# Attention over 16 groups of four heads: row maxima reduced two PSUM banks at a time, value products issued in parts of at most 256 columns

## The chip, the cores and the metric

The kernel runs on one core of one Trainium2 chip. A time is the device time of one launch in microseconds, a median over repeated runs. A profile is one execution of the same program recorded by the hardware profiler; its times below are microseconds from the first instruction.

## The reference, cut to what matters

The whole kernel is a two-layer transformer (attention with a feed-forward gate, then a retention layer with a gated mixture of experts). The change lies in the attention of the first layer, for 4 batches of 1024 tokens and 16 heads of width 8:

```python
S = 1024; NUM_HEADS = 16; D_K = 8
scores = einsum('bhnd,bhmd->bhnm', Q, K) / sqrt(D_K)      # Q, K with rotary positions
scores = where(tril(ones((S, S))), scores, -inf)
attn = softmax(scores, axis=-1)
head = einsum('bhnm,bhmd->bhnd', attn, V)
```

## The kernel before

Attention is one block with a hand-written order for each engine. Heads are taken four at a time: 16 groups x = 0 to 15 (4 batches, 4 quads of heads), pipelined over one another.

A softmax needs the maximum of each row before the exponentials. The kernel computes every score twice. First, `for_maximum` multiplies queries by keys with queries on the partitions, and VectorE (DVE) reduces each PSUM bank of up to 512 columns to one maximum a row (L766). A group has 40 such units; 8 of them hold two narrow heads in a bank. Then GpSimd (POOL) splits the negated maxima into two bf16 parts, TensorE (PE) turns them over (`turn_over`, L874), they are copied to SBUF as `negB` (L756) and placed by DMA as two extra rows of the queries (`place`). Second, `for_products` multiplies keys by queries with the keys on the partitions; the extra rows subtract the maxima inside the matmul. ScalarE (ACT) takes the exponential of that bank (L854) into the ring `probs`, which PE multiplies with the values (`products`, L959). A group has 40 such steps e = 0 to 39, in 12 slots j of (half c of the queries, key tile jt). Slots on the diagonal get four more small matmuls a head that add a mask (L899, L928); "masked" below means those.

PE interleaves the two kinds: each step issues one bank of scores for the exponentials (L921) together with one bank for the maxima of a later group (L892), in opposite halves of the array (`side_by_side`). So step e of group x stands beside unit e + 16 of group x + 1, or beside unit e - 24 of group x + 2 from e = 24 on. Widths match: 512 columns at steps 0 to 3, 12 to 23, 28 to 31 and 36 to 39, 384 at 4 to 7 and 24 to 27, and two heads of 128 or 256 columns at 8 to 11 and 32 to 35. Steps 0 to 11, 20 to 27 and 32 to 35 are masked.

PSUM has eight banks. Four (`mxb`, `RING`) take turns for the maxima, three (`st`, `BANKS`) for the exponentials, and one (`pv`) collects the value products of all four heads:

```python
LAG, DEEP = 5, 16
if n >= RING:
    pe.wait_ge(max_read, n - RING + 1)     # for_maximum: DVE has read this bank
if n >= BANKS:
    pe.wait_ge(exp_done, n - BANKS + 1)    # for_products: ACT has read this bank
```

`products(x, j)` is one block of four fp32 matmuls for slot j, as wide as the slot (512, 384, 256 or 128 columns), issued `LAG` steps after the slot's last step. A fp32 matmul is two records in the profile, so a block shows as x8. The 12 blocks of a group follow steps 0, 4, 7, 12, 14, 16, 20, 24, 28, 31, 36 and 38 (those after 0 and 4 belong to the group before). When a half of the queries is complete, ACT copies `pv` out (`keep`, L841): after the exponential of step 16, and of step 4 for the previous group. The first product block of the next half (slot 4 after step 20, slot 0 after step 7) waits for that copy (`out_kept`).

Before group 0 there are 44 units of maxima alone and a turn-over, then 12 more units. After group 13 maxima are left for one group only, and group 15 has none; small work of the second layer (`output_projection`, `turn_rows`) stands inside it.

Of the kernel before, what the change touches and what calls it, by code (L numbers as in the profile page):

```python
# [23 lines left out]
ACT = mybir.ActivationFunctionType  # L24
AX = mybir.AxisListType

P = 128
# [561 lines left out]
def attention(nc, A, groups, second, kept_until):  # L589
# [24 lines left out]
    LAG, DEEP = 5, 16  # L614
# [8 lines left out]
    order = prologue + [u for x in range(NQ) for u in stream(x)]  # L623
    place_of = {u: n for n, u in enumerate(order)}

# [9 lines left out]
    with Space(nc) as m:  # L635
        ps = m.psum("psB")
        mxb = [ps[:, i, :] for i in range(RING)]
# [26 lines left out]
        with nc.Block() as block:  # L664
            @block.sync
            def _(sp):
# [40 lines left out]
                sp.wait_ge(max_read, place_of[0, None] + 1)  # L707
                place(0)
                for x in range(NQ):
# [7 lines left out]
                    if x + 1 < NQ:  # L717
                        sp.wait_ge(max_read, place_of[x + 1, None] + 1)
# [21 lines left out]
            def _(dve):  # L740
# [4 lines left out]
                for n, (x, g) in enumerate(order):  # L745
                    if n == AHEAD:
# [3 lines left out]
                    if (x, g) == (SCALED, None):  # L750
                        reciprocals(0)
                    dve.wait_ge(max_done, n + 1)
                    if g is None:
                        if x >= 2:
                            dve.wait_ge(neg_placed[par], PLACED * (x // 2))
                        nc.vector.tensor_copy(neg[:, par, :], mxb[n % RING][0:64, 0:P]).then_inc(max_read, 1)  # L756
                        continue
                    heads, t, c = units[g]
                    w = max_width(t, c)
                    table, col = (mx, t) if c == 0 else (mx2, t - 4)  # L760
                    if len(heads) == 1:
                        dst, src = table[:, par, heads[0] % 2, heads[0] // 2, col:col + 1], mxb[n % RING][:, 0:w]
                    else:
                        dst = table[:, par, heads[0] % 2, :, col]
                        src = mxb[n % RING][:, 0:2 * w].rearrange("p (a w) -> p a w", w=w)
                    nc.vector.tensor_reduce(dst, src, AX.X, ALU.max).then_inc(max_read, 1)  # L766
                    if g == UNITS - 1:
                        dve.wait_ge(max_read, n + 1)
# [67 lines left out]
            def _(act):  # L836
# [5 lines left out]

                act.wait_ge(g2["in_loaded"], 16)
                nc.scalar.activation(second.gate[:, :, :], second.u[:, :, :], ACT.Silu).then_inc(g2["gated"], 1)
                act.wait_ge(g2["init"], 2)
                nc.scalar.activation(second.warm[:, :], second.eps[:, :], ACT.Exp)
                for x in range(NQ):
                    for e, (j, heads) in enumerate(steps):
                        n = UNITS * x + e
                        w = slot_width(j) * len(heads)  # L850
                        if n >= DEEP:
                            act.wait_ge(pv_done, read_up_to(n - DEEP))
                        act.wait_ge(st_done, n + 1)
# [1463 lines left out]
```

## Time and profile before

| | us |
|---|---|
| median of 3 runs | 1017.38 |
| lowest, highest | 1016.93, 1026.69 |
| span of the profiled execution | 1008.0 |
| median less span | 9.4 |
| attention, maxima of group 0 to the last copy | 117.5 to 539.2 |
| one group in the steady part | 23.84 |

The profiled execution has no time of its own beside the span; the 9.4 us are what lies around it by the median. The attention block is 42% of the span. The rest of the program is not touched.

### The profile page before, as it was taken

What the parts mean: (1) busy time and instruction counts of PE and PEld (TensorE: products, weight loads), DVE (VectorE), ACT (ScalarE), POOL (GpSimd) and SP (SyncE); (2) the same over time, 40 slices, a digit from 0 to 9 for tenths busy, and PEclk for the clock granted to TensorE, in tenths of its full rate; (3) what the DMA queues carried; (4) which work ended last, traced back from release to release, by engine and by line L of the source; (5) the groups of instructions that cost most, each with busy time, mean ns of one, the idle gap of its engine ahead of it and who ended that gap; (6) DMA issues with size and microseconds to landing.
All of it is one profiled execution on the core that took longest, in us unless ns stands there. A gap on an engine that the chain in (4) does not pass through costs nothing. (4 is left out here: it accounts for less than half of the span.)

```text
span 1008.0 us, 25094 instructions
## 1 busy us (share of the span) xinstructions
PE 874.2 (87%) x9373; PEld 464.7 (46%) x9374; DVE 816.2 (81%) x1699; ACT 725.7 (72%) x1493; POOL 289.1 (29%) x331
## 2 busy tenths in 40 slices
PE   4999899899999999999898898778999999979960
PEld 3666543334333333333344666533444444458850
DVE  6665499899999999999923766589999999928895
ACT  2666408788888888888784454478999999948851
POOL 4865311111111000000003656500344443005560
PEclk9999859999999999999999888768999999989995
DMA  5579851644445353330004899695354643546637
GB/s 167 223 267 331 280 133 42 205 101 105 110 98 125 89 123 84 68 69 14 13 24 127 277 317 301 226 241 101 67 118 94 114 89 54 136 142 189 206 119 252
DMA packets 121560, 147.20 MB, mean 146 GB/s; under 512 B 19213, under 2 KB 81242, under 8 KB 120800
## 3 DMA queue, kind: packets, MB, share of 16 engines
q1 hardware_dynamic: 116064, 133.74, 48.0%
q0 software_dynamic: 5376, 11.85, 4.1%
q8 instruction: 76, 1.25, 0.5%
q14 instruction: 44, 0.36, 0.1%
HBM read 77.63 MB, written 69.54 MB: 146 GB/s over the span
## 5 line engine op out<-in xcount | busy, mean ns | idle before, releaser
L854 ACT ACTIVATE probsB<-psB 128x512 f32<-128x512 f32 (+2 forms) x640 | 310.0, 566 | 87.1 <-PE psB L928 61.5
L766 DVE TENSOR_REDUCE mxB<-psB 128x1 f32<-128x512 f32 (+2 forms) x448 | 256.9, 642 | 11.1 <-PE psB L892 8.3
L921 PE MATMUL psB<-q_groups,k_groups 64*128 64x512 bf16 (+3 forms) x768 | 205.8, 330 | 16.6 <-DVE mxB L766 8.3
L892 PE MATMUL psB<-k_groups,q_groups 64*128 64x512 bf16 (+3 forms) x768 | 217.0, 344 | 2.8 <-PEq L293 1.7
L959 PE MATMUL psB<-probsB,vB 128*32 128x512 f32 (+3 forms) x1536 | 164.5, 500 | 0.7 <-ACT probsB L854 0.5
L1725 ACT ACTIVATE psD<-psD 128x896 f32<-128x896 f32 (+2 forms) x192 | 153.4, 799 | 12.9 <-PE psD L1779 12.7
L921 PEld LDWEIGHTS psB<-q_groups,k_groups 64*128 64x128 bf16 x768 | 67.5, 94 | 161.2 <-ACT probsB L854 140.3
L1656 DVE TENSOR_REDUCE sumsD<-psD 128x1 f32<-128x128 f32 (+3 forms) x256 | 113.2, 481 | 11.8 <-PE psD L1802 9.4
L899 PE MATMUL psB<-hideB,chooseB 64*128 64x128 bf16 (+1 forms) x1024 | 115.1, 210 | 0.0
L1779 PE MATMUL psD<-k_groups,q_groups 64*128 64x512 bf16 (+3 forms) x384 | 104.4, 343 | 12.3 <-ACT psD L1725 5.6
L766 DVE TENSOR_REDUCE mx2B<-psB 128x1 f32<-128x384 f32 (+2 forms) x192 | 104.4, 594 | 8.5 <-PE psB L899 6.9
L928 PE MATMUL psB<-hide_laterB,chooseB 64*128 64x64 bf16 (+1 forms) x1024 | 109.7, 205 | 0.0
L815 POOL TENSOR_SCALAR partsB<-mxB 128x32 f32<-128x32 f32 x16 | 4.6, 290 | 346.7 <-DVE mxB L769 346.7
L928 PEld LDWEIGHTS psB<-hide_laterB,chooseB 64*128 64x128 bf16 x1024 | 88.6, 95 | 19.8 <-issue 1.4
L899 PEld LDWEIGHTS psB<-hideB,chooseB 64*128 64x128 bf16 x1024 | 92.2, 98 | 9.9 <-issue 3.9
L1711 POOL DMA_INDIRECT slot_x<-xD,indexR x64 | 64.4, 1006 | 77.8 <-DVE sumsD L1656 39.5
L1667 DVE TENSOR_TENSOR keptD<-psD,causalD 128x512 f32<-128x512 f32 x128 | 82.5, 680 | 0.3 <-PE psD L1798 0.2
L892 PEld LDWEIGHTS psB<-k_groups,q_groups 64*128 64x128 bf16 x768 | 69.0, 95 | 13.4 <-DVE mxB L766 9.2
L1960 POOL DMA_INDIRECT back<-zE,toE x40 | 44.3, 1107 | 86.8 <-DVE zE L2147 76.7
L1779 PEld LDWEIGHTS psD<-k_groups,q_groups 64*128 64x128 bf16 x384 | 29.8, 96 | 80.8 <-ACT psD L1725 47.4
L1802 PE MATMUL psD<-k_groups,q_groups 64*128 64x128 bf16 (+3 forms) x256 | 64.8, 314 | 0.9 <-DVE keptD L1667 0.9
L1798 PE MATMUL psD<-q_groups,k_groups 64*128 64x128 bf16 x512 | 49.0, 225 | 6.8 <-DVE sumsD L1656 6.2
(227 smaller groups left out, 1504.5 us busy)
## 6 DMA issues: line engine op xcount, KB each, us to landing
v<-vaugA SPq DMA_DIRECT2D x4, 2048.0 KB, 8.9
vB<-v SPq DMA_DIRECT2D x16, 512.0 KB
q_groups<-q SPq DMA_DIRECT2D x32, 200.0 KB
k_groups<-k SPq DMA_DIRECT2D x32, 200.0 KB
q_groups<-q SPq DMA_DIRECT2D x32, 192.0 KB
k_groups<-k SPq DMA_DIRECT2D x32, 192.0 KB
back<-emptyB POOLq DMA_DIRECT2D x16, 256.0 KB, 3.8
o<-outB SPq DMA_DIRECT2D x128, 32.0 KB, 1.8
```

Of the source, the lines that this page charges most:

```text
L766: nc.vector.tensor_reduce(dst, src, AX.X, ALU.max).then_inc(max_read, 1)
L854: nc.scalar.activation(probs[:, n % DEEP, 0:w], st[n % BANKS][:, 0:w], ACT.Exp, scale=DH ** -0.5).then_inc(exp_done, 1)
L892: ins = nc.tensor.matmul(bank[:, to:to + w], q[half[r], s, hq // 2, t * P:t * P + P], k[half[r], s, hq // 2, HALF * c:HALF * c + w], start ...
L899: ins = nc.tensor.matmul(bank[:, to - P + ROWS * part:to], choose[half[r], part, :], hide[half[r], part, ROWS * part:P], start=False, stop ...
L921: ins = nc.tensor.matmul(bank[:, to:to + w], k[half[r], s, hq // 2, jt * P:jt * P + P], q[half[r], s, hq // 2, i0:i0 + w], start=True, sto ...
L928: ins = nc.tensor.matmul(bank[:, to:to + ROWS * (part + 1)], choose[half[r], part, :], hide_later[half[r], part, 0:ROWS * (part + 1)], sta ...
L959: ins = nc.tensor.matmul(pv[VW * hq:VW * hq + VW, HALF - w:HALF], v[:, s, jt, VW * hq:VW * hq + VW], probs[:, (UNITS * x + at) % DEEP, to: ...
L1656: ins = V.tensor_reduce(sums[:, s, unit:unit + 1], src[:, at:at + P * t], AX.X, ALU.add, apply_absolute_value=True)
L1667: V.tensor_tensor(dst[:, :, :, half, :], piece_bank[n % PIECE_RING].rearrange("p (t a i) -> p t a i", t=2, a=2), causal[:, None, None, :]. ...
L1725: nc.scalar.activation(src, src, ACT.Abs, accum_out=sums[:, s, unit:unit + 1]).then_inc(score_read, 1)
L1779: ins = nc.tensor.matmul(score[n % SCORE_RING][:, cols], q[r, s, hq // 2, P * t:P * t + P], k[r, s, hq // 2, cols], start=True, stop=True)
L1802: ins = nc.tensor.matmul(bank[:, at:at + P * t], q[r, s, hq // 2, P * t:P * t + P], k[r, s, hq // 2, 0:P * t], start=True, stop=True)
```

## The change

- Two maxima banks form a slot of the ring. `for_maximum` waits for a slot at its first bank only; DVE makes one reduction over both banks (20 a group for 40), and frees both at once.
- `turn_over` writes into the ring of the exponentials (`st`, three banks) and no longer into that of the maxima. Its copy to `negB` moves from DVE to ACT, `keep_negated`, in front of the exponential of step 28. Semaphore counts follow (`st_place`).
- A slot's products come in parts of at most 256 columns: 512 as two of 256, 384 as two of 192. That makes 20 blocks a group for 12. They follow the odd steps, one a pair of steps, from the fourth step after a slot's last one on (`LAG` 4): 256 columns after steps 1, 3, 5, 7, 9, 17, 19, 21, 23, 25, 27, 29, 35 and 37; 192 after 11, 13, 31 and 33; 128 after 15 and 39.
- `keep` now stands after the exponentials of steps 17 and 5. The first block of the next half follows steps 19 and 7 and waits for `out_kept` as before.

```diff
-    LAG, DEEP = 5, 16
+    SLOT = 2
+    LAG, DEEP, PART = 4, 16, HALF // 2
+    chunks = [(j, i, -(-slot_width(j) // PART)) for j in range(SLOTS_B) for i in range(-(-slot_width(j) // PART))]
+    issue_at, free = [], 1
+    for j, _, _ in chunks:
+        at = max(free, last_step[j] + LAG)
+        issue_at.append(at)
+        free = at + 2
+    HALF_AT = max(at for at, (j, _, _) in zip(issue_at, chunks) if j == 3)
+    END_AT = issue_at[-1] - UNITS
...
-        mxb = [ps[:, i, :] for i in range(RING)]
+        mxb = ps[:, 0:RING, :]
...
-                    dve.wait_ge(max_done, n + 1)
-                    if g is None:
-                        if x >= 2:
-                            dve.wait_ge(neg_placed[par], PLACED * (x // 2))
-                        nc.vector.tensor_copy(neg[:, par, :], mxb[n % RING][0:64, 0:P]).then_inc(max_read, 1)
-                        continue
+                    dve.wait_ge(max_done, SLOT * (m + 1))
...
+                    both = mxb[:, SLOT * m % RING:SLOT * m % RING + SLOT, :]
...
-                        dst, src = table[:, par, heads[0] % 2, heads[0] // 2, col:col + 1], mxb[n % RING][:, 0:w]
+                        dst, src = table[:, par, :, heads[0] // 2, col], both[:, :, 0:w]
...
+                def keep_negated(x):
+                    at = st_place[x, None]
+                    if x >= 2:
+                        act.wait_ge(neg_placed[x % 2], PLACED * (x // 2))
+                    act.wait_ge(st_done, at + 1)
+                    nc.scalar.copy(neg[:, x % 2, :], st[at % BANKS][0:64, 0:P]).then_inc(exp_done, 1)
...
-                        if e == last_step[3] + LAG:
+                        if e == HALF_AT:
                             keep(x, 0)
-                        if e == LAG - 1 and x:
+                        if e == END_AT and x:
                             keep(x - 1, 1)
...
-                    if n >= RING:
-                        pe.wait_ge(max_read, n - RING + 1)
+                    if n >= RING and n % SLOT == 0:
+                        pe.wait_ge(max_read, (n - RING) // SLOT + 1)
...
-                def products(x, j):
+                def products(x, j, i, parts_of):
...
+                    part = w // parts_of
+                    if i == 0:
+                        pe.wait_ge(exp_done, st_place[x, last_step[j]] + 1)
...
+                        if jt == 0 and x + c:
+                            pe.wait_ge(out_kept, 2 * x + c)
...
-                        if waiting and due(*waiting[0]) <= UNITS * x + e:
-                            products(*waiting.pop(0))
+                        if due[0][0] == UNITS * x + e:
+                            products(*due.pop(0)[1])
```

On PE, at steps 15 to 20 of a group in the steady part (L921 and L892 are the two scores of a step, L959 the products), the order before is:

```order
L959 MATMUL psB<-probsB,vB 32x128 x4
L921 MATMUL psB<-q_groups,k_groups 128x512
L892 MATMUL psB<-k_groups,q_groups 128x512
L921 MATMUL psB<-q_groups,k_groups 128x512
L892 MATMUL psB<-k_groups,q_groups 128x512
L959 MATMUL psB<-probsB,vB 32x256 x4
L921 MATMUL psB<-q_groups,k_groups 128x512
L892 MATMUL psB<-k_groups,q_groups 128x512
L921 MATMUL psB<-q_groups,k_groups 128x512
L892 MATMUL psB<-k_groups,q_groups 128x512
L921 MATMUL psB<-q_groups,k_groups 128x512
L892 MATMUL psB<-k_groups,q_groups 128x512
```

and after the change, from step 16 on (L947, L918 and L988 are the lines that were L921, L892 and L959):

```order
L988 MATMUL psB<-probsB,vB 32x128 x4
L947 MATMUL psB<-q_groups,k_groups 128x512
L918 MATMUL psB<-k_groups,q_groups 128x512
L947 MATMUL psB<-q_groups,k_groups 128x512
L918 MATMUL psB<-k_groups,q_groups 128x512
L988 MATMUL psB<-probsB,vB 32x256 x4
L947 MATMUL psB<-q_groups,k_groups 128x512
L918 MATMUL psB<-k_groups,q_groups 128x512
L947 MATMUL psB<-q_groups,k_groups 128x512
L918 MATMUL psB<-k_groups,q_groups 128x512
L988 MATMUL psB<-probsB,vB 32x256 x4
```

Before, three steps follow the block of slot 3 and a fourth (masked) comes before the block of 512 columns of slot 4; after, a block stands behind every second step, and the first half of slot 4 stands two steps behind slot 3.

On ACT, from step 20 of one group to step 19 of the next (L841 is `keep`), before:

```order
L854 ACTIVATE probsB<-psB 128x512 x10
L854 ACTIVATE probsB<-psB 128x384
L841 COPY outB<-psB 128x512
L854 ACTIVATE probsB<-psB 128x384 x3
L854 ACTIVATE probsB<-psB 128x256 x2
L854 ACTIVATE probsB<-psB 128x512 x7
L841 COPY outB<-psB 128x512
L854 ACTIVATE probsB<-psB 128x512 x7
```

and after (L879 the exponentials, L856 `keep`, L863 `keep_negated`):

```order
L879 ACTIVATE probsB<-psB 128x512 x10
L879 ACTIVATE probsB<-psB 128x384 x2
L856 COPY outB<-psB 128x512
L879 ACTIVATE probsB<-psB 128x384 x2
L879 ACTIVATE probsB<-psB 128x256 x2
L879 ACTIVATE probsB<-psB 128x512 x8
L856 COPY outB<-psB 128x512
L879 ACTIVATE probsB<-psB 128x512 x6
L879 ACTIVATE probsB<-psB 128x384 x4
L863 CAST negB<-psB 64x128
```

Each `keep` stands one exponential later, and the copy of the negated maxima is now in this queue, behind the 384-wide exponentials of steps 24 to 27.

## Rows read from the trace of the kernel before

**Rows 1.** The page, part 1, one engine: busy time, share, instructions.

```profile
PE 874.2 (87%) x9373; PEld 464.7 (46%) x9374; DVE 816.2 (81%) x1699; ACT 725.7 (72%) x1493; POOL 289.1 (29%) x331
```

**Rows 2.** Busy time, PE clock, DMA in four stretches.

```profile
core 0: us, PE busy (x) PEld busy (x) DVE busy (x) ACT busy (x) POOL busy (x), PEclk, DMA share, GB/s
125.00:140.00 15.00, 14.47 (x75) 6.47 (x74) 14.91 (x29) 0.00 (x0) 0.00 (x0) 0.50 0.76 178
...
286.10:310.00 23.90, 22.45 (x322) 9.19 (x322) 22.67 (x44) 20.21 (x43) 3.36 (x8) 1.00 0.46 106
...
500.60:538.60 38.00, 35.19 (x333) 14.26 (x333) 10.07 (x34) 28.35 (x60) 1.87 (x2) 0.96 0.33 90
```

**Rows 3.** The turn-over (L874) by tile: count, durations ns, first and last start.

```profile
L874 PE MATMUL psB<-identC,partsB x11: 270/271/272, 238.4 to 476.8; 128*64 128x128 f32 x11
```

**Rows 4.** Waits of one group, 262.3 to 286.1: total, times, longest.

```profile
PEld psB L921 <- ACT probsB L854: 9.0, 14, 0.9
```

**Rows 5.** DVE: four reductions in a row (timeline), and a 1024-element reduction (groups).

```profile
311.40 2.46 DVE L766 TENSOR_REDUCE mxB<-psB 128x1 f32<-128x512 f32 x4
...
L2095 DVE TENSOR_REDUCE msE<-sqE 128x128 f32<-128x1024 f32 x4 | 4.9, 1220 | 0.1
```

**Rows 6.** Timeline of PE, steps 15 to 20: start, us, instructions.

```profile
277.63 0.42 PE L959 MATMUL psB<-probsB,vB 128*32 128x128 f32 x8
277.99 0.39 PE L921 MATMUL psB<-q_groups,k_groups 64*128 64x512 bf16 x1
...
278.23 0.39 PE L921 MATMUL psB<-q_groups,k_groups 64*128 64x512 bf16 x1
...
278.55 0.64 PE L959 MATMUL psB<-probsB,vB 128*32 128x256 f32 x8
279.12 0.39 PE L921 MATMUL psB<-q_groups,k_groups 64*128 64x512 bf16 x1
...
279.35 0.73 PE L921 MATMUL psB<-q_groups,k_groups 64*128 64x512 bf16 x2
279.70 0.39 PE L892 MATMUL psB<-k_groups,q_groups 64*128 64x512 bf16 x1
280.68 0.39 PE L921 MATMUL psB<-q_groups,k_groups 64*128 64x512 bf16 x1 [0.59 <-DVE mxB L766]
```

**Rows 7.** Timeline of ACT over the same steps.

```profile
277.58 2.06 ACT L854 ACTIVATE probsB<-psB 128x512 f32<-128x512 f32 x4 [0.17 <-PE psB L921]
279.50 0.62 ACT L841 COPY outB<-psB 128x512 f32<-128x512 f32 x1
279.97 2.13 ACT L854 ACTIVATE probsB<-psB 128x512 f32<-128x512 f32 x4
```

**Rows 8.** Timeline, steps 3 and 4; then steps 21 to 27 and the turn-over.

```profile
270.79 0.38 PE L921 MATMUL psB<-q_groups,k_groups 64*128 64x512 bf16 x1
...
271.40 0.33 PE L921 MATMUL psB<-q_groups,k_groups 64*128 64x384 bf16 x1
...
282.08 0.39 PE L921 MATMUL psB<-q_groups,k_groups 64*128 64x512 bf16 x1
...
282.65 1.96 ACT L854 ACTIVATE probsB<-psB 128x512 f32<-128x512 f32 x4 [0.56 <-PE psB L928]
...
282.69 0.38 PE L921 MATMUL psB<-q_groups,k_groups 64*128 64x512 bf16 x1
...
283.30 0.33 PE L921 MATMUL psB<-q_groups,k_groups 64*128 64x384 bf16 x1
...
283.65 1.07 PE L959 MATMUL psB<-probsB,vB 128*32 128x512 f32 x8
284.55 0.17 DVE L769 TENSOR_TENSOR mxB<-mxB,mx2B 128x16 f32<-128x16 f32 x1
...
284.65 0.33 PE L921 MATMUL psB<-q_groups,k_groups 64*128 64x384 bf16 x1
...
285.16 0.32 PE L921 MATMUL psB<-q_groups,k_groups 64*128 64x384 bf16 x1
...
286.12 0.27 PE L874 MATMUL psB<-identC,partsB 128*64 128x128 f32 x1 [0.55 <-ACT probsB L854]
```

More of the change, by code:

```diff
@@ L613, in attention @@
     RING, BANKS = 4, 3
-    LAG, DEEP = 5, 16
+    SLOT = 2
[6 more added lines that the diff above has]
+        free = at + 2
+    assert all(at % 2 for at in issue_at) and issue_at[0] + UNITS >= free
+    HALF_AT = max(at for at, (j, _, _) in zip(issue_at, chunks) if j == 3)
+    END_AT = issue_at[-1] - UNITS
     def stream(x):
@@ L622, in attention @@
     prologue = [(0, g) for g in range(AHEAD)] + stream(-1)
-    order = prologue + [u for x in range(NQ) for u in stream(x)]
+    sequence = prologue + [u for x in range(NQ) for u in stream(x)]
+    order = [u for u in sequence if u[1] is not None]
     place_of = {u: n for n, u in enumerate(order)}
+    st_order = [(0, None)]
+    for x in range(NQ):
+        turned_at = next((e for e, u in enumerate(stream(x)) if u[1] is None), None)
+        for e in range(UNITS):
+            st_order += [(x + 1, None)] * (e == turned_at) + [(x, e)]
+    st_place = {u: n for n, u in enumerate(st_order)}
     def offset(heads, hq, w):
@@ L743, in reciprocals @@
                     nc.vector.reciprocal(second.rden[:, b, :], second.den[:, b, :]).then_inc(g2["rden_ready"], 1)
-                for n, (x, g) in enumerate(order):
-                    if n == AHEAD:
+                for m in range(len(order) // SLOT):
+                    x, g = order[SLOT * m]
+                    if SLOT * m == AHEAD:
                         nc.vector.memset(empty[:, :, 0:D + 1], 0.0).then_inc(emptied, 1)
@@ L846, in _ @@
                 nc.scalar.activation(second.warm[:, :], second.eps[:, :], ACT.Exp)
+                keep_negated(0)
                 for x in range(NQ):
                     for e, (j, heads) in enumerate(steps):
[L849 removed]
+                        n, at = UNITS * x + e, st_place[x, e]
                         w = slot_width(j) * len(heads)
+                        if st_order[at - 1] == (x + 1, None):
+                            keep_negated(x + 1)
                         if n >= DEEP:
                             act.wait_ge(pv_done, read_up_to(n - DEEP))
[L853 to L854 removed]
+                        act.wait_ge(st_done, at + 1)
+                        nc.scalar.activation(probs[:, n % DEEP, 0:w], st[at % BANKS][:, 0:w], ACT.Exp,
                                              scale=DH ** -0.5).then_inc(exp_done, 1)
[L856 removed]
+                        if e == HALF_AT:
                             keep(x, 0)
[L858 removed]
+                        if e == END_AT and x:
                             keep(x - 1, 1)
@@ L912, in for_products @@
                     w = slot_width(j)
[L913 removed]
+                    n = st_place[x, e]
                     if n >= BANKS:
@@ L991, in _ @@
                         side_by_side(for_maximum(x, g))
-                waiting = []
+                due = [(UNITS * x + at, (x, *chunk)) for x in range(NQ) for at, chunk in zip(issue_at, chunks)]
                 for x in range(NQ):
@@ L996, in _ @@
                     for e, (j, heads) in enumerate(steps):
-                        both = [for_products(x, e)]
                         if todo and todo[0][1] is None:
                             turn_over(todo.pop(0)[0])
+                        both = [for_products(x, e)]
                         if todo:
@@ L1011, in _ @@
                     assert not todo
-                for y in waiting:
-                    products(*y)
+                for _, chunk in due:
+                    products(*chunk)
 def between_layers(nc, A, groups, L, second, order, kept_until):
```

50 lines of the change are left out of this document (21 added, 29 removed).

## The prediction, made before the changed kernel ran

> **What bounds the kernel now.** The page comes first: no engine is full over the span, PE is fullest at 87% [rows 1]. The change lies in the attention, so the busy times by stretch come next. One steady group shows PE busy 22.45 of 23.90 us, DVE 22.67, ACT 20.21, at the full clock of 2.4 GHz [rows 2]. Two engines look full, and from this view alone one would take DVE, whose instructions are cut by half, for the bound. The turn-overs give the period: 11 of them from 238.4 to 476.8, 23.84 us a group [rows 3]. The list of waits names ACT 14 times a group in front of PE's loads of weights [rows 4], but a load idles there while a product block still streams, so those 9.0 us are no measure. What decides is the distance between starts on PE, compared with what the same piece takes when nothing holds it.
>
> The pieces are regular. An unmasked step takes 0.23 us (279.12 to 279.35) [rows 6]; two masked ones of 512 take 0.61 (282.08 to 282.69) [rows 8]. A product block of 128 columns takes 0.36 (277.63 to 277.99), one of 256 takes 0.57 (278.55 to 279.12), one of 512 takes 1.00 (283.65 to 284.65) [rows 6, 8]. That is a line: 0.145 us plus 0.00167 a column, so 0.465 for 192 and 0.785 for 384. The step in front of a block takes 0.32 and not 0.23 (278.23 to 278.55) [rows 6], so getting into a block costs 0.09 more.
>
> Against these times a group has about 2.6 us in which PE stands still. 0.87 of it lies at the copy `keep`: step 18 takes 0.35 and step 19 0.98 (279.70 to 280.68) where 0.23 would do each [rows 6], since ACT spends the time from 279.50 to 279.97 on the copy and frees the three banks late [rows 7]. 0.31 lies at step 23, which takes 0.61 (282.69 to 283.30): ACT had run dry during a block of 512, starts step 21's bank 0.57 after PE began it, and needs about 0.6 more. 0.31 lies at step 3 in the same way (270.79 to 271.40). 0.71 lies at the turn-over, where step 27 takes 0.96 (285.16 to 286.12) and the two before it 0.51 together (284.65 to 285.16) [rows 8], because the chain of last reduction, combination, POOL is late. The starts of the group's other steps leave some 0.4 in pieces of at most 0.1, of which 0.25 lie at steps 38 to 2, again behind a block of 512. So PE's own work is about 23.84 - 2.6 = 21.2 us a group. **DVE holds PE up only at the turn-over.** Four reductions of 512 take 2.46 us, last one 0.68, so they start 0.593 apart [rows 5]; over the 40 of mixed widths that is 21.6 us, under the period.
>
> **The change part by part, a steady group.**
> DVE: a pair of 512 takes 1.19 us now. A reduction of 1024 elements takes 1.22 and not 2 x 0.68 [rows 5]; its start-to-start should be 0.085 less, as for the small ones, 1.13. So one pair saves 0.06 us, 20 pairs 1.2 us, and a small copy goes as well. DVE drops to some 20.4 us. This reduction reads SBUF; that two PSUM banks cost the same is not in the trace. Bounds: 1.07 (the slope alone) and 1.36 (two full durations). I take 1.13. All of it lies beside PE's work and is worth nothing by itself.
> The Trainium skill, VectorE: DVE Perf Modes, section on the TRN2 errata, gives a PSUM read a fixed 120 cycles, 0.125 us an instruction; by it 20 fewer would save 2.5 us and not 1.2. The trace's spacing of 0.593 for 512 columns speaks for 0.06, and even 2.5 would be hidden in the same way.
>
> Products: 12 blocks sum to 6 x 1.00 + 2 x 0.785 + 2 x 0.57 + 2 x 0.36 = 9.43 us. 20 blocks are 14 x 0.57 + 4 x 0.465 + 2 x 0.36 = 10.56. That is +1.13, and eight more changes from scores to products at 0.10 (0.09 into it, 0.01 on the first step after it) give +0.8. Together **+1.95 us a group on PE**, with nothing to hide it, since PE sets the period. 192 and the second half of a slot are no rows of the trace; bounds +1.6 and +2.3.
> The Trainium skill, TensorE: Matmul & The Clock Gate, Part 2, says that loads of weights are pulled ahead of running matmuls. If the edges of a block were hidden so, the split would be free; what it would give is a rival below. The trace speaks against it, with 0.145 us of every block that no column accounts for.
>
> Stalls. With a block of at most 256 behind every second step, an unmasked pair lasts 0.23 + 0.32 + 0.57 = 1.11 us, a masked one about 1.26. ACT starts a bank some 0.48 us after PE does (0.57 masked) and holds it 0.60, at 0.48 apart [rows 7, 8]: the third step from it needs the bank 1.3 us or more after, it is free at 1.14 to 1.23. So both 0.31 stalls go (-0.62) and those of steps 38 to 2 (-0.25). At the turn-over, step 23 starts at t; the pair's reduction starts at t + 0.54, ends at t + 1.75, and the chain needs 1.57 more (284.55 to 286.12) [rows 8]: t + 3.36. PE is there at t + 3.32, since four blocks now lie between. So -0.66 of the 0.71.
> At `keep` after step 17, with step 16 at T: the exponential of 17 starts at T + 0.96, the copy at T + 1.44, and ends at T + 2.04 (0.47 behind the exponential, 0.60 long) [rows 7]. The block behind step 19 waits for it and would be ready at T + 1.65. That is a **new wait** of 0.44 us on PE, and all later steps queue behind it. In the run before it, pairs with blocks of 128 and 192 take PE 0.9 to 1.0 us where DVE needs 1.13, so PE meets a slot not yet read, 0.15 in all. 0.87 becomes 0.59: -0.28. `keep` after step 5 does the same with 384-wide banks: block ready at 1.77, copy done at 2.0: +0.25 where there was no stall. `keep_negated` costs ACT some 0.3 us of its 3 us of slack; one bank of `st` is gone for a step, and step 30 comes 0.6 us after the copy is done: nothing.
>
> Sum: +1.95 - 0.62 - 0.25 - 0.66 - 0.28 + 0.25 = **+0.39 us a group**, 24.2 us. Over the 14 periods with all three kinds of work, +5.4 us.
>
> **Prologue and end.** 56 units run alone at half clock, 1.2 GHz, with DVE busy 14.91 of 15 us [rows 2]: DVE is the bound there. 28 pairs save 0.06 each, 1.7 us; the first reduction waits for a second bank and the last is longer (+0.7): -1.0. In the last 38 us PE has scores of one kind alone, ACT is busy 28.35 us [rows 2]; 11 more blocks cost 2.6 us and blocks of 256 stop ACT running dry, worth 1 to 4 us. I take 0. Sum: +4.4 us on the span of 1008.0, so 1012.4; with the 9.4 around it 1021.8 against 1017.38. The rest of the program is not touched.
>
> **The rivals.**
> *New waits add up (slower).* Every place where I count a wait of 0.1 to 0.4 rests on 0.05 to 0.2 us of slack. If the copies of both halves come one exponential later than reckoned (+0.48 each), or the slot of two banks is freed late at the 10 unmasked pairs (0.07 each), a group takes 0.7 to 1.7 more: 25.2, +1.4 x 14 = 19, so 1036. For it: the chain ACT, PE, ACT is visible at every `keep` [rows 6, 7]. Against: ACT and DVE each get 3 us of slack. It is slower by 1% from +0.7 a group on.
> *The waits vanish.* If the copy starts as soon as its block is done, and no slot is late, the group is 21.2 + 1.95 + 0.15 = 23.3: -0.5 x 14 = -8 us, 1009.
> *The split is free.* Then 21.2 and about 0.9 of waits: 22.1, -1.7 x 14 = -24 us and so 993. Only this case needs a fixed cost that the trace shows 12 times a group to go away.
> *DVE was the bound after all.* PE's stalls would then be DVE's doing, and the period falls with DVE's work, by 1.5 to 2: 22.1, 993. Against: the stalls sit where ACT is late, and DVE falls idle in the same group for 1.2 us.
> *It does not do what it says*: the order shows 20 blocks and 20 reductions a group, so this has no chance of its own.
>
> **How the numbers follow.** Forecast (+1 to +9) 0.58; new waits 0.25; waits vanish 0.10; free split 0.04; DVE the bound 0.03. A measurement of this kernel tells 1%, 10 us, from no change. Of the forecast some 0.05 lies above 1%, of the vanishing waits 0.03 below: faster 0.10, same 0.61, slower 0.29. The range takes in the bounds of the split (-5 and +5), the vanishing waits and the nearer half of the new waits: 1006 to 1034.
>
> **What would show it.** Right: products of 256 columns 0.57 us from start to start; turn-overs 24.2 apart; step 27 no longer long; a gap of 0.4 us in front of the block behind step 19, released by the copy; DVE busy about 20.5 a group with its idle time doubled or more. Wrong: turn-overs under 23.5 apart (split cheaper, or no waits), or DVE still busy 22 us (two banks read more slowly). The whole would be wrong if the clock did not stay at full rate in the groups, which nothing in the change suggests.

## The result, and the profile after

The change makes the kernel slower: 1032.63 us (median of 4 runs, 1029.57 to 1037.07) against 1020.06 before in the same rounds. The ratio is 1.0144, interval 1.0100 to 1.0188. Run again later beside other kernels (e9) it was 1.0151, interval 1.0106 to 1.0196. The prediction, 1021.8 in a range of 1006 to 1034, was too low: it had +4.4 us where the medians differ by 12.6 and the ratio makes 14.6. Its chance for "slower by over 1%" was 0.29.

The profiled execution has a span of 1031.8 us, 23.8 more than the one before. Less than that is the change's. Cut at the first score of the maxima and the end of the last copy of the products, the two traces give:

| stretch, us | before | after | difference | forecast |
|---|---|---|---|---|
| start to the first score (untouched) | 117.47 | 119.44 | +2.0 | 0 |
| first score to the first turn-over | 24.47 | 24.85 | +0.4 | -1.0 |
| first to last turn-over, 15 periods | 358.7 | 371.2 | +12.5 | +5.4 |
| last turn-over to the last copy | 38.5 | 39.4 | +0.8 | 0 |
| the rest of the program (untouched) | 468.8 | 477.0 | +8.2 | 0 |

The attention takes 13.7 us more, which agrees with the 14.6 us that 1.0144 makes. The untouched rest is not constant from one profiled execution to the next: over the profiles of this study it took 467.8 to 479.5 us. So spans of single profiles are no measure here, and below the distances between turn-overs are read instead. A run also lasts 1.8 us more than its span (1033.61 and 1031.8), not the 9.4 that the prediction put around it: the profiled execution before was simply a quick one.

First the page of the changed kernel, part 1:

```profile
PE 889.8 (86%) x10397; PEld 481.6 (47%) x10398; DVE 800.8 (78%) x1363; ACT 737.7 (71%) x1509; POOL 289.3 (28%) x331
```

Against [rows 1], PE has 1024 matmuls more and is busy 15.6 us longer. DVE has 336 instructions fewer and is busy only 15.4 us less. By stretches (columns as in [rows 2]):

```profile
125.00:140.00 15.00, 9.06 (x68) 3.74 (x66) 13.95 (x15) 1.61 (x3) 0.00 (x0) 0.50 0.90 206
286.00:310.00 24.00, 23.36 (x381) 10.17 (x384) 21.00 (x21) 20.39 (x43) 3.31 (x7) 1.00 0.44 101
```

In a steady stretch of 24 us PE is now busy 23.36 us where it was 22.45 in 23.90 [rows 2], and DVE 21.00 where it was 22.67. The roles are clear: PE is full, DVE is not. The turn-over's line by tile (columns as in [rows 3]):

```profile
L900 PE MATMUL psB<-identC,partsB x16: 298/298/423, 144.3 to 515.5; 128*64 128x128 f32 x16
```

and of DVE's groups by form (count, busy us, mean ns, idle before them) the widest:

```profile
L781 DVE TENSOR_REDUCE mxB<-psB 128x2 f32<-128x1024 f32 x148 | 172.8, 1219 | 6.5 <-PE psB L918 4.9 <-PE psB L925 1.4
```

The turn-overs from 144.3 to 515.5 are 24.75 us apart on average; ten of the fifteen distances are 24.56 to 24.61, and the first three, the eighth and the last are longer, 24.82 to 25.65. Steady period: **24.56 us for 23.84**. A reduction of two banks takes 1.219 us, what a 1024-element one took in SBUF [rows 5].

The timeline of PE at steps 14 to 20, to be held against [rows 6]:

```profile
309.34 0.37 PE L947 MATMUL psB<-q_groups,k_groups 64*128 64x512 bf16 x1
...
309.88 0.43 PE L988 MATMUL psB<-probsB,vB 128*32 128x128 f32 x8
310.47 0.37 PE L947 MATMUL psB<-q_groups,k_groups 64*128 64x512 bf16 x1 [0.17 <-ACT probsB L879]
...
311.01 0.64 PE L988 MATMUL psB<-probsB,vB 128*32 128x256 f32 x8
311.61 0.37 PE L947 MATMUL psB<-q_groups,k_groups 64*128 64x512 bf16 x1
...
311.84 0.38 PE L947 MATMUL psB<-q_groups,k_groups 64*128 64x512 bf16 x1
312.65 0.64 PE L988 MATMUL psB<-probsB,vB 128*32 128x256 f32 x8 [0.44 <-ACT outB L856]
313.22 0.39 PE L947 MATMUL psB<-q_groups,k_groups 64*128 64x512 bf16 x1
```

Two gaps stand out. The block of 128 columns is followed by step 16 after 0.59 us (309.88 to 310.47), where it was 0.36. And the block behind step 19 starts 0.81 us after the step's first score (311.84 to 312.65), where 0.31 is normal: PE waits for `keep`. DVE and ACT at the same place:

```profile
309.11 4.61 DVE L781 TENSOR_REDUCE mxB<-psB 128x2 f32<-128x1024 f32 x4
...
309.81 2.22 ACT L879 ACTIVATE probsB<-psB 128x512 f32<-128x512 f32 x4
311.91 0.59 ACT L856 COPY outB<-psB 128x512 f32<-128x512 f32 x1
312.38 1.12 ACT L879 ACTIVATE probsB<-psB 128x512 f32<-128x512 f32 x2
```

Four two-bank reductions take 4.61 us, so they start 1.13 apart, and the first ends at 310.33. Step 16 needs that slot and starts 0.14 later. (The row of step 16 names ACT. The exponential whose bank step 16 takes is that of step 13, three banks back, and it had ended at 309.86; with single banks, in e2, this wait is gone.) The copy runs from 311.91 to 312.50, and the block starts 0.15 after it.

The turn-over is where the wait went away. In the changed kernel it follows a block, without a gap (the block of 256 takes its 0.57 us, 317.55 to 318.12):

```profile
317.55 0.64 PE L988 MATMUL psB<-probsB,vB 128*32 128x256 f32 x8
318.12 0.30 PE L900 MATMUL psB<-identC,partsB 128*64 128x128 f32 x1
```

### The profile page after: what moved, and what is told of

It is laid out like the page before. It is cut to its first block and busy times, and to the rows that moved or that the text cites. A ratio compares the mean times of both kernels' runs of the same rounds, so it can differ in the third digit from the quotient of the medians.

```text
span 1031.8 us, 26531 instructions
## 1 busy us (share of the span) xinstructions
PE 889.8 (86%) x10397; PEld 481.6 (47%) x10398; DVE 800.8 (78%) x1363; ACT 737.7 (71%) x1509; POOL 289.3 (28%) x331
## 5 line engine op out<-in xcount | busy, mean ns | idle before, releaser
L879 ACT ACTIVATE probsB<-psB 128x512 f32<-128x512 f32 (+2 forms) x640 | 318.9, 556 | 67.6 <-PE psB L954 55.9
L781 DVE TENSOR_REDUCE mxB<-psB 128x2 f32<-128x1024 f32 (+2 forms) x224 | 244.9, 1143 | 19.2 <-PE psB L925 13.1
L918 PE MATMUL psB<-k_groups,q_groups 64*128 64x512 bf16 (+3 forms) x768 | 205.4, 342 | 13.1 <-DVE mxB L781 9.5
L947 PE MATMUL psB<-q_groups,k_groups 64*128 64x512 bf16 (+3 forms) x768 | 207.2, 330 | 5.3 <-ACT probsB L879 3.0
L988 PE MATMUL psB<-probsB,vB 128*32 128x256 f32 (+2 forms) x2560 | 191.9, 372 | 11.0 <-ACT outB L856 10.7
L781 DVE TENSOR_REDUCE mx2B<-psB 128x2 f32<-128x768 f32 (+2 forms) x96 | 100.5, 1048 | 29.4 <-PE psB L925 28.4
L947 PEld LDWEIGHTS psB<-q_groups,k_groups 64*128 64x128 bf16 x768 | 64.9, 94 | 122.7 <-ACT probsB L879 101.4
L1803 PE MATMUL psD<-k_groups,q_groups 64*128 64x512 bf16 (+3 forms) x384 | 106.1, 350 | 11.7 <-ACT psD L1749 3.6
L925 PE MATMUL psB<-hideB,chooseB 64*128 64x128 bf16 (+1 forms) x1024 | 110.8, 210 | 0.0
L925 PEld LDWEIGHTS psB<-hideB,chooseB 64*128 64x128 bf16 x1024 | 88.3, 98 | 13.9 <-issue 2.2
L988 PEld LDWEIGHTS psB<-probsB,vB 128*32 128x32 f32 x2560 | 51.6, 108 | 78.6 <-ACT probsB L879 40.3
L918 PEld LDWEIGHTS psB<-k_groups,q_groups 64*128 64x128 bf16 x768 | 63.0, 95 | 20.8 <-DVE mxB L781 15.3
```

What stands on the lines that cost most here:

```text
L879: nc.scalar.activation(probs[:, n % DEEP, 0:w], st[at % BANKS][:, 0:w], ACT.Exp, scale=DH ** -0.5).then_inc(exp_done, 1)
L918: ins = nc.tensor.matmul(bank[:, to:to + w], q[half[r], s, hq // 2, t * P:t * P + P], k[half[r], s, hq // 2, HALF * c:HALF * c + w], start ...
L925: ins = nc.tensor.matmul(bank[:, to - P + ROWS * part:to], choose[half[r], part, :], hide[half[r], part, ROWS * part:P], start=False, stop ...
L947: ins = nc.tensor.matmul(bank[:, to:to + w], k[half[r], s, hq // 2, jt * P:jt * P + P], q[half[r], s, hq // 2, i0:i0 + w], start=True, sto ...
L988: ins = nc.tensor.matmul(pv[VW * hq:VW * hq + VW, col:col + part], v[:, s, jt, VW * hq:VW * hq + VW], probs[:, (UNITS * x + at) % DEEP, to ...
L1803: ins = nc.tensor.matmul(score[n % SCORE_RING][:, cols], q[r, s, hq // 2, P * t:P * t + P], k[r, s, hq // 2, cols], start=True, stop=True)
```

## The experiments

Each is told with its steady period, read as the distance between turn-overs in its profile, which is the same within 0.02 us over seven or more groups. The time of whole runs stands beside it. The median of the kernel before was 1012.33 in the rounds of e1 to e4, 1017.88 in those of e5 to e8 and 1018.92 in those of e9 to e11, so only ratios are compared across them. The ratios of e2 to e5 lie within one another's intervals, and e3's 1.0099 against 1.0144 is more than its period explains; what sets the variants apart from one another is read from the periods, and the ratios say only that each is slower or faster than the kernel before. e6, e7 and e8 ran once each.

| kernel | maxima | product blocks | period, us | attention, us | ratio to before (interval) |
|---|---|---|---|---|---|
| before | one bank | 12, whole | 23.84 | 421.7 | |
| changed | two banks | 20, parts | 24.56 | 435.4 | 1.0144 (1.0100 to 1.0188) |
| e1 | two banks | 12, whole, odd steps | 24.89 | 441.7 | 1.0201 (1.0143 to 1.0259) |
| e2 | one bank | 20, parts | 24.30 | 428.5 | 1.0106 (1.0074 to 1.0138) |
| e3 | two banks | 20, parts, copy first | 24.48 | 435.1 | 1.0099 (1.0072 to 1.0127) |
| e4 | two banks | 18 | 24.37 | 435.4 | 1.0093 (1.0065 to 1.0121) |
| e5 | one bank | 12, whole, odd steps | 24.31 | 433.1 | 1.0104 (1.0062 to 1.0145) |
| e6 | one bank | 12, in adjacent parts | 23.88 | 422.6 | one run, 1018.0 us |
| e7 | one bank, half read | 12, whole | 23.47 | 411.1 | one run, 1004.0 us |
| e8 | two banks | 20, parts, short copy | 23.98 | 429.8 | one run, 1023.6 us |
| e9 | two banks | 20, parts (changed again) | 24.57 | 434.9 | 1.0151 (1.0106 to 1.0196) |
| e10 | one bank | 12, turn-over at 30 | 23.57 | 419.5 | 0.9973 (0.9947 to 0.9999) |
| e11 | one bank | 12, turn-over at 32 | 23.59 | 416.6 | 0.9963 (0.9937 to 0.9989) |

### e1: product blocks whole again

```diff
-    LAG, DEEP, PART = 4, 16, HALF // 2
+    LAG, DEEP, PART = 4, 16, HALF
```

> The changed kernel with the value products whole again (12 blocks a group, up to 512 columns, behind odd steps), all else as in the change. Theory A (the split is what costs: PE has 23.3 us of its own work a group, 8 more blocks of 0.24 us each, and the copy waits): PE's own work falls to about 21.3 us, the turn-overs come 22.3 to 23.0 us apart for 24.56, and the time falls about 25 us below the changed kernel's, to below the kernel before. Theory B (the slots of two banks cost, since PE waits until both are read): the turn-overs stay at 24 us or more, since a pair of steps without a block now runs into a slot that is still being read.

The period rose to 24.89 us and the time to 1.0201. Theory A, that taking the parts back would give the 2 us of block edges back, is refuted for this arrangement. Its timeline of PE shows where the time goes, at steps 0 to 3:

```profile
300.49 0.37 PE L947 MATMUL psB<-q_groups,k_groups 64*128 64x512 bf16 x1
...
300.81 0.38 PE L947 MATMUL psB<-q_groups,k_groups 64*128 64x512 bf16 x1
...
301.63 0.37 PE L947 MATMUL psB<-q_groups,k_groups 64*128 64x512 bf16 x1 [0.35 <-DVE mxB L781]
```

Step 1 takes 0.82 us (300.81 to 301.63) for 0.30, and the release is DVE's. A pair without a block behind it lasts 0.6 us on PE, and DVE needs 1.13 for the pair before. The parts do add work to PE, but with slots of two banks they also spread PE's work so that it runs into fewer of DVE's reads.

### e2: maxima one bank at a time

```diff
-    SLOT = 2
+    SLOT = 1
-        bank = mxb[:, n // SLOT * SLOT % RING + heads[0] % 2, :]
+        bank = mxb[:, n % RING, :]
```

and one reduction a bank, as in the kernel before.

> The changed kernel with maxima reduced one bank at a time (40 reductions a group), the products in parts and the turn-over in the ring of the exponentials as in the change. Theory A: PE's blocks and the two waits for the copy stay, so the turn-overs come 24.3 to 24.7 us apart, as in the changed kernel, though DVE is busy some 1.2 us a group more. Theory B: without two-bank slots the 0.3 to 0.4 us of waits in front of steps 14 to 18 go and the period is 24.2 or less. If DVE's work mattered by itself (theory C, DVE a second bound), the period would rise to 25 or more.

24.30 us, against 24.56. So reading in pairs costs 0.26 us a group and gains nothing, though DVE does more work in e2. The number lies in theory A's range, and the 0.26 are theory B's mechanism: the two do not exclude one another. Theory C falls. The pieces show the waits for a slot gone: the block of 128 columns behind step 15 is followed by step 16 after 0.36 us again (309.25 to 309.61), and the gap in front of the block of step 19 is 0.6 us, the largest of the group:

```profile
310.98 0.38 PE L948 MATMUL psB<-q_groups,k_groups 64*128 64x512 bf16 x1
311.89 0.42 PE L989 MATMUL psB<-probsB,vB 128*32 128x256 f32 x4 [0.54 <-ACT outB L857]
```

The parts, with their new places and the turn-over in the other ring, cost 24.30 - 23.84 = 0.46 us.

### e3: the copy in front of the exponential

```diff
+                        if e == HALF_AT:
+                            keep(x, 0)
+                        if e == END_AT and x:
+                            keep(x - 1, 1)
                         act.wait_ge(st_done, at + 1)
                         nc.scalar.activation(probs[:, n % DEEP, 0:w], st[at % BANKS][:, 0:w], ACT.Exp,
                                              scale=DH ** -0.5).then_inc(exp_done, 1)
-                        if e == HALF_AT:
-                            keep(x, 0)
-                        if e == END_AT and x:
-                            keep(x - 1, 1)
```

> The changed kernel with the copy of the products (keep) in front of the exponential of steps 17 and 5 on ScalarE, where it stood behind it. Theory A: the copy starts when its block is done, 0.25 us sooner at step 17 and 0.15 sooner at step 5, so the gap in front of the block of step 19 falls from 0.52 to about 0.25 us and the one of step 7 from 0.27 to about 0.1: period 24.56 - 0.4 = 24.15 us, 6 us in all. If the gap is not the copy's doing, the period stays at 24.56.

The period fell to 24.48, by 0.08 and not 0.4. The gap at step 19 did shrink, from 0.50 to 0.35 us:

```profile
311.33 0.38 PE L947 MATMUL psB<-q_groups,k_groups 64*128 64x512 bf16 x1
311.99 0.64 PE L988 MATMUL psB<-probsB,vB 128*32 128x256 f32 x8 [0.28 <-ACT outB L856]
```

That of step 7 grew by 0.05, since ACT now stands idle 0.34 us until its block is done. The copy cannot start before the block is out of PE; its place in ACT's queue was a small part of the wait. The mechanism is right, its size was overrated.

### e4: only the blocks of 512 in parts

```diff
+    parts_in = [2 if slot_width(j) == HALF else 1 for j in range(SLOTS_B)]
-    chunks = [(j, i, -(-slot_width(j) // PART)) for j in range(SLOTS_B) for i in range(-(-slot_width(j) // PART))]
+    chunks = [(j, i, parts_in[j]) for j in range(SLOTS_B) for i in range(parts_in[j])]
```

> The changed kernel with the blocks of 384 columns whole and only those of 512 in two parts: 18 blocks a group for 20. The first block of slot 4 then still follows step 19, but the copy stands behind step 15. Theory A: 2 x 0.24 us less of PE's own work, and the wait of 0.52 us for the copy at step 19 goes: 24.56 - 1.0 = 23.55 us a group, 15 us less than the changed kernel. If edges of blocks cost nothing (the products' columns alone count), only the 0.5 of the wait goes: 24.05.

24.37 us, 0.19 less than the changed kernel and not 1.0. The wait of the block for the copy is gone, but another took its place at once:

```profile
312.71 0.38 PE L948 MATMUL psB<-q_groups,k_groups 64*128 64x512 bf16 x1
313.61 0.37 PE L948 MATMUL psB<-q_groups,k_groups 64*128 64x512 bf16 x1 [0.52 <-DVE mxB L782]
```

Steps 16 to 18 now come with no block behind 17, so step 17 takes 0.90 us and step 18 another 0.40. ACT's row shows the copy in that place, at 312.84 for 0.62 us, with the exponentials that should free banks behind it. Two waits overlap here. Step 18 itself waits for DVE: its slot of two banks is read until 0.14 us before it starts, while the exponential that it needs, of step 15, had ended 0.6 us before. Step 19 then waits for the exponential behind the copy. The second wait would stand without the first: in e5, with single banks, steps 17 and 18 take 0.35 and 0.98, 1.33 us for the 1.30 here. So the time lost is that of the stall of the kernel before [rows 6], back in a new place.

Over the whole attention e4's profile shows no gain on the changed kernel (435.4 us both): one of its distances between turn-overs is 28.44 us, with the granted clock at half for 3.4 us of it, where the changed kernel has 25.65.

### e5: one bank at a time and blocks whole

e1 and e2 together.

> The changed kernel with both parts undone but its placement kept: maxima one bank at a time, products whole, behind odd steps, and the turn-over in the ring of the exponentials. With e1, e2 and the changed kernel it makes a square of two by two. If paired reading costs through PE's waits for a slot and the parts are what hides them, the square shows an interaction: this kernel's period lies near the kernel before (23.84 us), 23.2 to 23.9, far under e1's 24.89. If the placement at odd steps is what is bad about e1, the period stays above 24.5. If it is under 23.6, this version beats both kernels.

24.31 us. With e1, e2 and the changed kernel it completes the square:

| period, us | 12 blocks whole | 20 blocks in parts |
|---|---|---|
| one bank | 24.31 | 24.30 |
| two banks | 24.89 | 24.56 |

Pairs cost 0.58 us with whole blocks and 0.26 with parts. At these odd places the parts cost nothing in the end: they add 2 us to PE's work and take 2 us of its waits. The 0.47 us to the kernel before's 23.84 lie in what all four share: blocks at odd steps with LAG 4, and the turn-over with its copy among the exponentials. No run has one without the other, but e5's timeline tells where the time is:

```profile
275.31 0.32 PE L948 MATMUL psB<-q_groups,k_groups 64*128 64x384 bf16 x1
...
275.97 0.33 PE L948 MATMUL psB<-q_groups,k_groups 64*128 64x384 bf16 x1 [0.25 <-ACT probsB L880]
...
289.98 0.63 PE L948 MATMUL psB<-q_groups,k_groups 64*128 64x512 bf16 x2
...
290.88 0.39 PE L948 MATMUL psB<-q_groups,k_groups 64*128 64x512 bf16 x1 [0.27 <-ACT probsB L880]
```

Step 6 takes 0.66 us (275.31 to 275.97) for 0.24, and step 30 takes 0.66 for 0.23: the fourth step since a block, 7 and 31, starts late, as steps 4 and 24 do in the kernel before [rows 8]. At their old places the whole blocks leave four runs of four wide steps (512 or 384 columns), at the odd ones six. The two new stalls are +0.85 us; the wait in front of the turn-over shrinks by 0.41, from step 27's 0.96 to step 26's stall of 0.31; every other stall of the kernel before stands within 0.03 us, some a step earlier. That makes up the 0.47, so in e5 it is the placing; the turn-over in its new ring shows no wait of its own. That the period would lie at 23.2 to 23.9 did not hold; that pairs and whole blocks harm one another did.

### e6: the parts directly behind one another

```diff
+                    parts_of = 2 if w > HALF // 2 else 1
+                    part = w // parts_of
+                    for i in range(parts_of):
                         for hq in range(4):
```

in `products` of the kernel before, with columns and flags as in the change.

> The kernel before with each product block of 512 or 384 columns issued as two parts directly behind one another, no scores between: the instructions of the change's parts without its moves. If the fixed cost of a block (0.145 us) is paid at the change between scores and products, an adjacent second part adds at most 0.05 us: 8 x 0.05 = 0.4 us at most, period 23.8 to 24.2. If it is a cost of every eight matmuls with their loads of weights, each adds 0.145: 8 x 0.145 = 1.2, period about 24.9.

23.88 us for 23.84. A block of 512 in two adjacent parts takes 1.01 us (292.90 to 293.91), as the whole one did:

```profile
292.90 1.07 PE L963 MATMUL psB<-probsB,vB 128*32 128x256 f32 x16
293.91 0.39 PE L921 MATMUL psB<-q_groups,k_groups 64*128 64x512 bf16 x1
```

So eight more matmul records with their loads of weights cost nothing. The 0.145 us of a block that no column accounts for is paid once for products that stand together, so at the change between products and scores. The Trainium skill, TensorEngine Tiling (Array Packing), Key Properties, says that changing the tiling mode drains TensorE. The trace agrees so far as each change has a price, some 0.24 us for a block's way in and out. That the price is such a drain is not shown: products and scores differ in their rows (128 and 64) and in their type (fp32 and bf16), and no run changes one alone.

### e7: half of DVE's work

```diff
-                        dst, src = table[...], mxb[n % RING][:, 0:w]
+                        dst, src = table[...], mxb[n % RING][:, 0:w // 2]
```

in the kernel before, the packed units likewise, with the exponential's scale at a thousandth.

> The kernel before with VectorE reducing only the left half of each bank (the maxima are of half the columns, and the exponential's scale is a thousandth, so the output is not the attention's; all instructions and waits stay). It takes about half of DVE's work away, 11 us a group. If DVE is not the bound (the prediction's reading), only the wait at the turn-over goes, 0.71 us: period 23.1. If DVE's work was the bound or helped to set it, the period falls to 22.3 or less, and the worth of the 20 reductions saved was more than nothing.

DVE's busy time fell to 15.49 us in 24, and the period from 23.84 to 23.47 only:

```profile
286.00:310.00 24.00, 22.98 (x335) 9.44 (x333) 15.49 (x44) 20.51 (x44) 3.31 (x7) 1.00 0.47 108
```

Every piece of PE's group is as it was within 0.03 us but one, the step in front of the turn-over:

```profile
300.69 0.32 PE L921 MATMUL psB<-q_groups,k_groups 64*128 64x384 bf16 x1
301.25 0.30 PE L874 MATMUL psB<-identC,partsB 128*64 128x128 f32 x1
```

It takes 0.56 for 0.96 us. Step 19 takes 0.98 us in e7 too, so the wait that its row puts down to DVE [rows 6] is ACT's. DVE was not the bound of the steady groups. It is the bound of the prologue: first score to first turn-over fell from 24.47 to 15.34 us, and DVE was busy 14.38 of 15.30 us there, 23.87 of 24.50 before. The granted clock was higher in e7's prologue too (0.89 for 0.52 on average), and no run separates the two.

### e8: a shorter copy

```diff
-                    nc.scalar.copy(out[:, c, :], pv).then_inc(out_kept, 1)
+                    cols = HALF if x < 2 or x == NQ - 1 else P
+                    nc.scalar.copy(out[:, c, 0:cols], pv[:, 0:cols]).then_inc(out_kept, 1)
```

in the changed kernel.

> The changed kernel in which the copy of the products out of PSUM takes 128 of the 512 columns in groups 2 to 14 (the rest of those outputs is left out). The copy falls from 0.59 to some 0.27 us. If the gaps in front of the blocks of steps 19 and 7 are the wait for this copy, they shrink by 0.3 and 0.27 us, to 0.2 and 0: period 24.56 - 0.55 = 24.0. If they come from a lack of free banks, they stay.

23.98 us, 0.58 less, as expected. The block of step 19 starts 0.49 us after its step for 0.81:

```profile
309.71 0.38 PE L948 MATMUL psB<-q_groups,k_groups 64*128 64x512 bf16 x1
310.20 0.64 PE L989 MATMUL psB<-probsB,vB 128*32 128x256 f32 x8
```

The new waits are waits for the copy. Without most of it the changed kernel would still be slower than the one before, by 0.14 us a group.

### e9: the changed kernel again

> The changed kernel itself, on the same chip and in the same rounds as e10 and e11. The steady period is 24.56 us again; the time is 1.0 to 1.8% over the kernel before. If it were within 0.5%, what was measured first would be the chip's and not the change's.

Period 24.57 us, ratio 1.0151. The first measurement holds.

### e10 and e11: the turn-over later, in the kernel before

```diff
-    AHEAD, DELAY = 16, 4
+    AHEAD, DELAY = 16, 6
```

and 8 in e11.

> The kernel before with the turn-over two steps later, in front of step 30 (DELAY 6 for 4). Halving DVE's work in e7 took 0.41 us off the step in front of the turn-over and left 0.30, though POOL was done 0.65 us before it. If the 0.41 is the wait for the chain of DVE and POOL, it goes: period 23.43, 6 us less in all. If it is a wait for ScalarE, it comes back at another step and the period stays at 23.84.

> The kernel before with the turn-over in front of step 32, right behind the block of step 31 (DELAY 8). If the other 0.30 us is TensorE's price for going from the scores of a step to the turn-over, it goes too, as in the changed kernel, where the turn-over follows a block: period 23.13, 10 us less than the kernel before. Against it: the copy, the DMA and the wait of the next group's first step have 4 us left for some 3.5; if they are late, a gap of 0.5 us or more stands in front of step 0 and the period is 23.6 or more.

e10 has a period of 23.57 us and a time of 0.9973 of the kernel before's (interval 0.9947 to 0.9999); e11 23.59 and 0.9963 (0.9937 to 0.9989). The 0.41 us of e7 is the wait for DVE and POOL. In both kernels step 27 takes 0.55 to 0.56 us, so all of it goes there, but some 0.14 come back elsewhere: in e10 in step 29, which now leads into the turn-over (0.32 for 0.23), and around it, in e11 at step 33 (0.43 for 0.28). The other 0.30 us did not go in e11, though its turn-over stands behind a block:

```profile
307.66 0.32 PE L921 MATMUL psB<-q_groups,k_groups 64*128 64x384 bf16 x1
308.21 0.39 PE L921 MATMUL psB<-q_groups,k_groups 64*128 64x512 bf16 x1
...
310.28 0.85 PE L959 MATMUL psB<-probsB,vB 128*32 128x384 f32 x8
311.06 0.30 PE L874 MATMUL psB<-identC,partsB 128*64 128x128 f32 x1
```

Step 27 still takes 0.55 us, now with no turn-over near. So this is not a price of the turn-over, as the expectation of e11 had it, but the late start of the fourth step since a block, as in front of steps 4 and 24. The program says why e7 shows it at the turn-over: PE's wait for the bank of step 28 (`for_products`) is issued before the turn-over, which so waits for ACT as well. e11 beats both kernels, by 0.4% and 1.8%.

## Why the prediction was wrong

**What held.** PE bounds the steady groups and DVE does not (e7). The pieces have the lengths that were read off: a block of 256 columns takes 0.57 us in the changed kernel, one of 192 takes 0.465, and a pair of banks costs DVE 1.13. The fixed cost of a block is the change between products and scores (e6), so the rival "the split is free", for parts with scores between them, falls, as does "DVE was the bound". The turn-over's wait went, and the block of step 19 waits for the copy, as foretold.

**Where it failed: the sum of the stalls, +0.39 us a group where +0.72 was measured.** By its terms:

| term, us a group | forecast | measured |
|---|---|---|
| slots of two banks not yet read | +0.15 | +0.38 |
| stalls of steps 38 to 2, gone | -0.25 | -0.05 |
| `keep` after step 17: old stall less new wait | -0.43 | -0.36 |
| `keep` after step 5 | +0.25 | +0.26 |
| stalls of steps 3 and 23, gone | -0.62 | -0.62 |
| wait in front of the turn-over, gone | -0.66 | -0.72 |
| eight more blocks with their edges | +1.95 | +1.82 |
| sum | +0.39 | +0.72 |

The measured column compares the same pieces of one steady group in the traces of the two kernels; the term of the blocks is what the others leave of 0.72 (the prediction's -0.28 for `keep` holds the -0.43 and the +0.15). Two terms were mis-sized, and they are the step that failed:

- *Slots of two banks, "0.15 in all".* In the changed kernel's group PE meets an unread slot for some 0.38 us that the same pieces of e2 do not have: 0.23 in front of step 16, 0.07 of step 0, 0.05 of step 14, the rest small. As the wait at step 19 is 0.1 longer in e2, its period is only 0.26 less. Steps 12 and 13 with their block of 192 take PE 1.00 us by themselves, steps 14 and 15 with their block of 128 take 0.89, and DVE needs 1.13 for each: 0.37 us together, of which 0.3 is waited on the spot. The prediction's own pieces (0.9 to 1.0 us against 1.13, twice) would have given 0.26 to 0.46.
- *The new wait at step 19, "0.44".* It is 0.50, since the block starts 0.15 us after the copy ends. The one of step 7 is 0.26, as reckoned (0.25). Together they are what e8 takes away in part.
- *The turn-over.* I had counted all the 0.96 us of step 27 but 0.25 as wait for the turn-over's chain. Only 0.41 is that (e7), 0.30 is a stall of the kind of steps 3 and 23 (e11). As both kinds go in the changed kernel, this misreading costs the sum nothing, by luck. The stall of step 3 also stands behind a block of 256 columns and not of 512, as the prediction had it.

*Stalls of steps 38 to 2, "-0.25".* The kernel before has only some 0.05 us of stall there:

```profile
268.92 0.39 PE L921 MATMUL psB<-q_groups,k_groups 64*128 64x512 bf16 x1
...
269.20 0.37 PE L921 MATMUL psB<-q_groups,k_groups 64*128 64x512 bf16 x1
...
269.61 0.64 PE L959 MATMUL psB<-probsB,vB 128*32 128x256 f32 x8
270.18 0.39 PE L921 MATMUL psB<-q_groups,k_groups 64*128 64x512 bf16 x1
...
270.79 0.38 PE L921 MATMUL psB<-q_groups,k_groups 64*128 64x512 bf16 x1
```

Steps 1 and 2 take 0.61 us (270.18 to 270.79), what the prediction itself gives for two masked steps. Step 0 takes 0.41, a masked step and the 0.09 in front of a block. Only step 39 is longer than its kind, 0.28 for 0.23. What was read as a stall is PE's own work, and it is still there after the change.

The edges of a block came 0.13 us a group cheaper than reckoned, which hid part of the error.

**What the prediction did not see.** Parts in their new places and pairs act on one another (e5's square). The placing at odd steps costs whole blocks 0.47 us (e5), and the parts fill its runs of steps without a block, which is why e2, with all the work of the parts, is no slower than e5. The stalls of the kernel before were each taken as a thing that a smaller block removes. The one at `keep` is rather work of ACT, 4 banks of 0.48 us and a copy of 0.47, that has to pass in some stretch of PE's order; e4 and e5 show it coming back where the copy then stands.

**The ends.** The prologue gained nothing (+0.4 for -1.0) though DVE bounded it before: at half clock DVE stands idle in front of pairs of masked banks until the second is done, and was busy 13.95 of 15 us where it was 14.91 [rows 2]:

```profile
125.34 3.49 DVE L781 TENSOR_REDUCE mxB<-psB 128x4 f32<-128x1024 f32 x3 [0.72 <-PE psB L925]
...
134.87 1.23 DVE L781 TENSOR_REDUCE mx2B<-psB 128x4 f32<-128x1024 f32 x1 [0.53 <-PE psB L925]
```

Fifteen full periods of the difference, not fourteen, fit the trace, and the groups off the steady period add 1.7 us. So 15 x 0.72 + 1.7 = 12.5 us stand where 5.4 was forecast. With the +0.8 of the end, where 0 was taken, the attention is 13.7 us longer for the +4.4 forecast.

The likeliest of the rivals was "new waits add up (slower)", with its threshold at +0.7 us a group. It came out just there: of the 0.33 us above the forecast 0.23 came through slots freed late and 0.08 through the copies, as that rival had it. The missing gain at steps 38 to 2, 0.20, it did not name; the cheaper edges and the turn-over took 0.19 back.

## What to carry to other kernels

Where several engines pass banks around, count every engine's work in the stretch between two large pieces, not over the period: a stall is work of another engine that needs a place, and taking away the wait that shows it moves it to the next. Saving instructions on an engine with slack is worth nothing, and if it is paid for by handing over two buffers at once, it costs as soon as the other engine is the faster one for two pairs in a row. A small move of a late chain (the turn-over four steps later) gave more than both rewrites.

## What the runs showed of the hardware that was not expected

- A product block costs 0.145 us plus 0.00167 us a column, and 0.09 us more in front, at every change between 64-row bf16 scores and 128-row fp32 products; two blocks without scores between pay it once (1.01 us for 16 matmul records of 256 columns, and 1.00 for 8 of 512).
- From the end of another engine's read to the start of the waiting matmul it is 0.14 to 0.15 us in the changed kernel's rows at full clock (DVE 310.33 to 310.47, ACT's copy 312.50 to 312.65). After an exponential it is shorter: in the kernel before, that of step 17 ends at 280.63 (279.97 and 0.66 us) and step 20, which needs its bank, starts at 280.68. Why they differ is open.
- A two-bank reduction of 1024 elements from PSUM takes 1.219 us, as one of 1024 elements from SBUF does (1.220 [rows 5]), and starts 1.13 after the last. How far apart they start from SBUF no row shows.
- The part of the program that no kernel of this study changes took 467.8 to 479.5 us in its profiles, a spread of 11.7 us, nearly as much as the change cost the attention (13.7).
